# Half-height low products of the shared layer paired across two parts, and the refinement's second layer as products of rounded parts, in a kernel of attention, two feed-forward blocks and a routed iteration

## What is computed

```python
v, integrated = 0, x
for _ in range(2):                                   # NUM_ITER
    ctx = concat([integrated, v])
    shared_ctrl = gelu(ctx @ w_s1 + b_s1) @ w_s2 + b_s2          # shared layer, hidden 64
    x_shared, v_shared = inl(shared_ctrl, integrated, v, mu)
    hidden = gelu(ctx @ w1[expert] + b1[expert])                  # 2 of 8 experts, hidden 64
    ctrl = hidden @ w2[expert] + b2[expert]
    x_r, v_r = inl(ctrl, ...)                                     # weighted over the two
    x_next = sw * x_shared + (1 - sw) * x_r
    v_next = sw * v_shared + (1 - sw) * v_r
    halt = sigmoid(gelu(x_next @ w_h1 + b_h1) @ w_h2 + b_h2)
    refined = gelu(x_next @ w_f1 + b_f1) @ w_f2 + b_f2            # refinement, 128 -> 256 -> 128
    integrated = integrated + halt * refined * integration_weight
    v = v_next
```

## Time and profile before

| | us |
|---|---|
| median of 3 runs | 353.34 (353.13 to 353.79) |
| the profiled execution | 352.54 |
| its span in the profile | 350.8 |
| PE busy | 320.6 (91%), 1498 instructions |
| PEld busy | 225.9 (64%) |
| DVE busy | 276.4 (79%), 548 instructions |
| ACT busy | 194.8 (56%), 307 instructions |
| POOL busy | 35.4 (10%) |
| granted TensorE clock | 0.981 of full speed |
| chain that ended last, by engine | PE 68%, DVE 15%, ACT 7%, issue 5% |

### The profile page before, as it was taken

One profiled execution on the slowest core, in us unless ns is written; L12 is line 12 of the kernel. 1 busy time (PEld: TensorE's weight loads), 2 busy tenths in 40 slices (PEclk: granted clock), 3 DMA queues, 4 the chain that ended last, 5 costly groups with the idle time before them and its releaser, 6 DMA issues.

```text
span 350.8 us, 4318 instructions
## 1 busy us (share of the span) xinstructions
PE 320.6 (91%) x1498; PEld 225.9 (64%) x1498; DVE 276.4 (79%) x548; ACT 194.8 (56%) x307; POOL 35.4 (10%) x41
## 2 busy tenths in 40 slices
PE   4989999899898777896998999999999999999996
PEld 4654787445464454574675777777777777776763
DVE  0556767645757668969999999999997996999694
ACT  3500026285746274497778784866746846635743
POOL 0040020211111110709000100000000000000000
PEclk9989999999999679999999999999999999999999
DMA  7999930000000000000000100101000100000001
GB/s 266 421 429 298 325 153 0 0 2 2 0 2 0 0 1 2 0 0 2 1 0 0 33 0 2 30 0 30 2 1 0 32 1 0 32 0 0 32 0 60
DMA packets 11444, 18.91 MB, mean 54 GB/s; under 512 B 416, under 2 KB 8864, under 8 KB 10144
## 3 DMA queue, kind: packets, MB, share of 16 engines
q1 hardware_dynamic: 10848, 17.60, 14.5%
q0 software_dynamic: 576, 1.05, 1.8%
HBM read 16.55 MB, written 1.05 MB: 50 GB/s over the span
## 4 chain that ended last, share of the span: by engine, by line
PE 68%; DVE 15%; ACT 7%; issue 5%; POOL 2%; DMA 2%; SPq 0%; DVEq 0%; ACTq 0%; POOLq 0%
PE ps L1255 63%; DVE zz L860 3%; POOL lrs L381 2%; DVE lst L845 2%; PE ps L1352 2%; DMA ctxT<-in_ctxT 2%; PE ps L1331 1%; ACT hid L535 1%; DVE st L745 1%; ACT ring L483 1%; ACT L646 1%; DVE lmv L848 1%; DVE a L761 1%; PE ps L1437 1%; DVE kv L1144 1%
## 5 line engine op out<-in xcount | busy, mean ns | idle before, releaser
L1255 PE MATMUL ps<-hm_even,ew_hi 128*128 128x512 f32 (+1 forms) x160 | 51.0, 417 | 1.1 <-issue 1.1
L1255 PE MATMUL ps<-hm_odd,ew_hi 128*128 128x512 f32 (+1 forms) x164 | 51.6, 416 | 0.0
L1255 PEld LDWEIGHTS ps<-hm_odd,ew_hi 128*128 128x128 f32 (+1 forms) x164 | 28.7, 189 | 5.8 <-issue 0.5
L1255 PEld LDWEIGHTS ps<-hm_even,ew_hi 128*128 128x128 f32 (+1 forms) x160 | 27.9, 188 | 6.3 <-issue 1.2
L535 ACT ACTIVATE hid<-ps,pB 128x512 f32<-128x512 f32 x32 | 21.6, 687 | 13.4 <-PE ps L1255 12.8
L1255 PE MATMUL ps<-hm_odd,ew_lo 128*128 128x512 f32 (+1 forms) x80 | 28.3, 391 | 0.0
L1255 PE MATMUL ps<-hm_even,ew_lo 128*128 128x512 f32 (+1 forms) x80 | 28.3, 390 | 0.0
L860 DVE TENSOR_SCALAR zz<-ps,lmv,lrs 128x128 f32<-128x128 f32 x48 | 16.4, 404 | 9.4 <-POOL lrs L381 9.2
L381 POOL TENSOR_TENSOR lrs<-lve,mhalf 128x4 f32<-128x4 f32 x12 | 12.2, 1017 | 106.0 <-DVE lve L850 106.0
L1255 PE MATMUL ps<-x_hi,w1x_hi 128*128 128x512 f32 x40 | 18.9, 474 | 4.3 <-ACT ring L503 2.2
L945 DVE SCALAR_TENSOR_TENSOR ring<-ring,pB,hid 128x1024 f32<-128x1024 bf16 x16 | 20.5, 1282 | 2.0 <-ACT hid L535 1.3
(11 more groups left out here) (291 smaller groups left out, 739.4 us busy)
## 6 DMA issues: line engine op xcount, KB each, us to landing
ring<-in_fc1b SPq DMA_DIRECT2D x4, 1024.0 KB, 17.8
ring<-in_fc2a SPq DMA_DIRECT2D x4, 1024.0 KB, 8.9
packC<-in_packC SPq DMA_DIRECT2D x1, 1152.0 KB, 9.3
pB<-in_packB SPq DMA_DIRECT2D x1, 1141.5 KB, 10.1
ctxT<-in_ctxT SPq DMA_DIRECT2D x2, 512.0 KB, 6.7
xtok<-in_xtok SPq DMA_DIRECT2D x1, 1024.0 KB, 9.4
xT<-in_xT SPq DMA_DIRECT2D x1, 1024.0 KB, 11.4
a<-in_fc1a SPq DMA_DIRECT2D x1, 1024.0 KB, 13.4
```

What stands on the lines that cost most here:

```text
L1255: return pe.matmul(out, lhsT, rhs, start=start, stop=stop)
```

## The change

**Part one, from step 2 on (`PAIRED = 2`).** In the second part of a step (GATE in steps 2 and 3, ALPHA in steps 4 to 7) the ninth half-height product is left out. It is issued instead in BETA's `row_tiles`, right behind BETA's own, on the bottom half of the array and into the next group's shared bank. For that the bottom half needs the high part of the shared tile in rows 64 to 127, which before held only the low part. So ScalarE's two gelus of 128 rows become three of 64: `hsf` (full, rows 64 to 127, in the memory of `hsh`), `hs_hi` (rounded, rows 64 to 127, in a place of its own) and `hsh` (rounded, rows 0 to 63). VectorE's subtraction makes the low part in place from the first two. `hsu` rises twice a step, and `hsu_at(s)` gives its value after the last gelu of step s. BETA's `row_tiles` has two more waits: for the squashing of the group before, whose banks are written, and for `hsu`.

**Part two, refinements 4, 5 and 6 (`SPLIT`).** `refine1` writes each half of fh twice, rounded (`fh_hi`) and in full. VectorE subtracts (`refine_low`, behind `halt_low`, in steps 5, 6 and 7). `refine_b` makes six products of parts in place of two in full. The weights are split once, in step 4.

**Besides.** The full gelu of h1 covers its 32 rows alone; the four semaphores of GpSimd's accumulating transfers become one, and each transfer waits for the one before.

The diff, cut (allocations and the renaming of `xsum` left out):

```diff
+        SPLIT = range(NCH, STEPS - 1)
+        PAIRED = 2
+        def hsu_at(s):
+            return s + 1 + max(0, s + 1 - PAIRED)
...
                     if j == HT:
                         if s >= 1:
                             act.wait_ge(sem("hsl"), s)
-                        act.activation(hs, hid_bank(s, HT), ACT.Gelu, bias=W("bs1")).then_inc(sem("hs"), 1)
-                        if s >= 2:
+                        if s >= PAIRED:
 
                             act.wait_ge(sem("part_ps"), group(s - 1, 0))
-                        act.activation(hsh[:, s % 2, :], hid_bank(s, HT), ACT.Gelu, bias=W("bs1"))\
-                            .then_inc(sem("hsu"), 1)
+                            out, half = hid_bank(s, HT), slice(64, 128)
+                            act.activation(hsf[half, s % 2, :], out[half], ACT.Gelu, bias=W("bs1")[half])\
+                                .then_inc(sem("hs"), 1)
+                            act.activation(hs_hi[s % 2][half, :], out[half], ACT.Gelu, bias=W("bs1")[half])\
+                                .then_inc(sem("hsu"), 1)
+                            act.activation(hsh[0:64, s % 2, :], out[0:64], ACT.Gelu, bias=W("bs1")[0:64])\
+                                .then_inc(sem("hsu"), 1)
...
+                    if s in SPLIT:
+                        act.activation(fh_hi[:, j, :], bank[7 - j], ACT.Gelu, bias=W("bf1", j, j + 1))\
+                            .then_inc(sem("fhi"), 1)
                     act.activation(fh[:, j, :], bank[7 - j], ACT.Gelu, bias=W("bf1", j, j + 1))\
                         .then_inc(sem("fhg"), 1)
...
-                act.activation(h1, bank[7], ACT.Gelu, bias=W("bh1")).then_inc(sem("h1f"), 1)
+                act.activation(h1[32:64], bank[7][32:64], ACT.Gelu, bias=W("bh1")[32:64]).then_inc(sem("h1f"), 1)
...
+                if s == NCH:
+                    act.wait_ge(sem("hm"), (HT - 1) * (s + 1))
+                    act.activation(wf2_hi, W("wf2"), ACT.Copy).then_inc(sem("wf2"), 1)
...
+                if s >= PAIRED:
+                    dve.wait_ge(sem("hsu"), hsu_at(s) - 1)
+                    dve.tensor_tensor(hsh[half, s % 2, :], hsf[half, s % 2, :], hs_hi[s % 2][half, :].bitcast(F),
+                                      ALU.subtract).then_inc(sem("hsl"), 1)
...
+            def refine_low(s):
+
+                dve.wait_ge(sem("fhg"), 2 * s + 2)
+                dve.wait_ge(sem("fhi"), 2 * (s - SPLIT[0]) + 2)
+                dve.tensor_tensor(fh_lo[:, :, :], fh, fh_hi[:, :, :].bitcast(F), ALU.subtract).then_inc(sem("flo"), 1)
...
                 if s >= 1:
                     halt_low(s - 1)
+                if s - 1 in SPLIT:
+                    refine_low(s - 1)
...
                     mm(lo, w_hi[top, :], m[top, 1, 0, :], start=False, stop=not first)
-                    mm(hi, w_hi[bot, :], m[bot, 1, 0, :], start=False, stop=not first)
-                    return mm(sh, ws2_lo[top, o], h[top, :], start=first, stop=not first)
+                    last = mm(hi, w_hi[bot, :], m[bot, 1, 0, :], start=False, stop=not first)
+                    if paired and part == parts(s)[1]:
+                        return last
+                    if paired and rows_last:
+
+                        pe.wait_ge(sem("squash"), 2 * n)
+                        pe.wait_ge(sem("hsu"), hsu_at(s))
+                    last = mm(sh, ws2_lo[top, o], h[top, :], start=first, stop=not first)
+                    if paired and rows_last:
+                        p = parts(s)[1]
+                        mm(bank[3 * (n % 2)], ws2_lo[bot, p * D:(p + 1) * D], hs_hi[s % 2][bot, :], stop=False)
+                    return last
...
+                if s in SPLIT:
+                    pe.wait_ge(sem("wf2"), 2)
+                    pe.wait_ge(sem("flo"), s - SPLIT[0] + 1)
                 for j in range(2):
-                    last = mm(bank[7], W("wf2", j * 128, (j + 1) * 128), fh[:, j, :],
-                              start=j == 0, stop=j == 1)
+                    w = slice(j * 128, (j + 1) * 128)
+                    if s in SPLIT:
+                        mm(bank[7], wf2_hi[:, w], fh_hi[:, j, :], start=j == 0, stop=False)
+                        mm(bank[7], wf2_lo[:, w], fh_hi[:, j, :], start=False, stop=False)
+                        last = mm(bank[7], wf2_hi[:, w], fh_lo[:, j, :], start=False, stop=j == 1)
+                    else:
+                        last = mm(bank[7], W("wf2")[:, w], fh[:, j, :], start=j == 0, stop=j == 1)
                 last.then_inc(sem("f2_ps"), 1)
                 if s + 3 < STEPS:
-                    pe.wait_ge(sem("hsu"), s + 4)
+                    pe.wait_ge(sem("hsu"), hsu_at(s + 3))
```

More of the change, by code:

```diff
@@ L115, in build @@
         bank = [ps[:, i * CH:(i + 1) * CH] for i in range(8)]
+        hB_at = (nc.sbuf_base + 31) // 32 * 32
         hB_f = sb("hB", [128, 2 * FT * CH])
@@ L147, in build @@
         vtok = vtok_f.rearrange("p (b d) -> p b d", b=B)
+        wz_at = (nc.sbuf_base + 31) // 32 * 32
         wz = sb("wz", [128, 3 * CH])
@@ L206, in build @@
         hs = wz[:, 2 * CH:3 * CH]
+        hsh_at = (nc.sbuf_base + 31) // 32 * 32
         hsh = sb("hsh", [128, 2, CH], FR)
+        hsf = nc.alloc_sbuf_tensor_at("hsf", [128, 2, CH], F, offset=hsh_at)
+        hs_hi = tuple(nc.alloc_sbuf_tensor_at(n, [128, CH], FR, offset=at)
+                      for n, at in (("hs_hi_even", wz_at + 4 * 2 * CH), ("hs_hi_odd", zz_at + 4 * 3 * CH)))
         hm = (wz[:, 0:2 * CH].rearrange("p (k n) -> p k n", k=2),
@@ L238, in build @@
         wh2s = sb("wh2s", [128, 1], FR)
+        wf2_hi, wf2_lo = (placed(n, 2 * D, ring_at + 4 * (IDX0 + i * 2 * D)) for i, n in enumerate(("wf2_hi", "wf2_lo")))
+        fh_hi, fh_lo = (nc.alloc_sbuf_tensor_at(n, [128, 2, CH], FR, offset=at)
+                        for n, at in (("fh_hi", hB_at), ("fh_lo", zz_at)))
         xn_hi, xn_lo = placed("xn_hi", CH, ctxT_at + 4 * 3 * CH), placed("xn_lo", CH, zz_at + 4 * 2 * CH)
@@ L415, in _ @@
                 pool.wait_ge(sem("xi"), s + 1)
-                pool.dma_start(xT[:, ck(s)], xi[:, ck(s)], accum_op=ALU.add).then_inc(sem(f"xsum_{s}"), 16)
+                if s:
+                    pool.wait_ge(sem("xsum"), 16 * s)
+                pool.dma_start(xT[:, ck(s)], xi[:, ck(s)], accum_op=ALU.add).then_inc(sem("xsum"), 16)
         @block.scalar
@@ L516, in hidden_gelus @@
                             act.wait_ge(sem("hsl"), s)
-                        act.activation(hs, hid_bank(s, HT), ACT.Gelu, bias=W("bs1")).then_inc(sem("hs"), 1)
-                        if s >= 2:
+                        if s >= PAIRED:
                             act.wait_ge(sem("part_ps"), group(s - 1, 0))
-                        act.activation(hsh[:, s % 2, :], hid_bank(s, HT), ACT.Gelu, bias=W("bs1"))\
-                            .then_inc(sem("hsu"), 1)
+                            out, half = hid_bank(s, HT), slice(64, 128)
[6 more added lines that the diff above has]
+                        else:
+                            act.activation(hs, hid_bank(s, HT), ACT.Gelu, bias=W("bs1")).then_inc(sem("hs"), 1)
+                            act.activation(hsh[:, s % 2, :], hid_bank(s, HT), ACT.Gelu, bias=W("bs1"))\
+                                .then_inc(sem("hsu"), 1)
                     else:
@@ L998, in shared_halves @@
             def shared_halves(s):
+                half = slice(64, 128)
                 dve.wait_ge(sem("hs"), s + 1)
-                dve.wait_ge(sem("hsu"), s + 1)
-                dve.tensor_tensor(hsh[64:128, s % 2, :], hs[64:128, :], hsh[64:128, s % 2, :].bitcast(F),
-                                  ALU.subtract).then_inc(sem("hsl"), 1)
+                if s >= PAIRED:
+                    dve.wait_ge(sem("hsu"), hsu_at(s) - 1)
+                    dve.tensor_tensor(hsh[half, s % 2, :], hsf[half, s % 2, :], hs_hi[s % 2][half, :].bitcast(F),
+                                      ALU.subtract).then_inc(sem("hsl"), 1)
+                else:
+                    dve.wait_ge(sem("hsu"), s + 1)
+                    dve.tensor_tensor(hsh[half, s % 2, :], hs[half, :], hsh[half, s % 2, :].bitcast(F),
+                                      ALU.subtract).then_inc(sem("hsl"), 1)
             ln_stats("ffn", 0)
@@ L1198, in last_refine @@
                     link(dve.tensor_scalar(th[:, cut(i)], th[:, cut(i)], 1.0, iwh[:, 0:1], ALU.add, ALU.mult))
-                dve.wait_ge(sem(f"xsum_{NCH - 1}"), 16)
+                dve.wait_ge(sem("xsum"), 16 * NCH)
                 for i in range(2):
@@ L1214, in refine @@
                 else:
-                    dve.wait_ge(sem(f"xsum_{c}"), 16)
+                    dve.wait_ge(sem("xsum"), 16 * (c + 1))
                     dve.tensor_tensor(res[:, ck(c)], xT[:, ck(c)], rr, ALU.add).then_inc(sem("res"), 1)
@@ L1241, in _ @@
                     hidden_masked(s + 1, s + 2 < STEPS)
+                if s == NCH:
+                    dve.wait_ge(sem("wf2"), 1)
```

(4 more changed lines are left out.)

2 lines of the change are left out of this document (added).

## The result

The changed kernel takes 361.33 us (median of 6 executions, 358.96 to 362.19) beside 353.24 (352.53 to 356.08, also 6) for the one before: ratio 1.0186, interval 1.0140 to 1.0232. The forecast of 357.8 had the sign and missed the size; 361.33 lies above its range of 354.8 to 359.4. The profiled execution took 362.19, its span 360.0 against 350.8. In every ratio of this document the executions more than 1.5% above the fastest of their own kernel are left out (four of ten in delay_full, further down, at most two elsewhere).

What follows compares the result with a forecast made beforehand. TensorE was taken to bound up to step 6's tanh, VectorE from there to xn_lo and again at the end. Terms 1.90 + 1.26 + 1.26 = +4.42 us on the median 353.34 gave 357.8, range 354.8 to 359.4.

Steps and rivals of the forecast that it cites:

- Step 1's wait for the third gelu: Step 1: expand_3's weights load on TensorE waits for the last shared-tile gelu, a loss of 0.59 us.
- The h1s waits in steps 2 to 5: refine_b's halt product on TensorE waits for hsu, 0.50 us lost a step, +2.00 in all.
- I take 0.59 us more a step: ScalarE: three 64-row gelus for two full ones, each costing as much as a full one, 0.59 us more a step.
- Three slots in steps 3 to 5: TensorE: the second part's low product, paired with BETA's, saves a 0.23 us slot in each step, -0.69.
- Sum to the tanh: All terms from step 1 up to step 6's tanh, where TensorE sets the pace: +1.90 us.
- fh_lo in step 6: VectorE's added 128x1024 subtraction, in the stretch without a pause before xn_lo: +1.26 us.
- in step 7: The same VectorE subtraction, queued after h1s and ahead of all that the end needs: +1.26 us.
- The gelus of the first layer and the halting weights: Step 7: two added refine1 gelus on ScalarE, with halt_a beginning after two, just fit: nothing, 0.1 at the other end.
- The clock in the gap: Rival: TensorE's clock falls in step 7's 2.5 us gap ahead of refinement; products could double, +4.7, 362.5 us; chance 6%.

Runs made afterwards that it cites:

- delay_full: The kernel before, with the 32-row h1 gelu and one idle 128x1024 VectorE subtraction in step 7's turn, no pairing or split; ratio to before 1.0022.
- third_gelu: The changed kernel without the split and with the low products unpaired as before, its three 64-row gelus kept; ratio to the kernel before 1.0123.
- fill: The whole changed kernel plus eight idle TensorE products in step 7's gap ahead of refinement; ratio to the kernel before 1.0144.
- early_pair: The changed kernel without the split, its shared tile read by one full-height gelu and the rounded parts copied from that; 354.05 us, ratio to before 1.0009.
- split_only: The changed kernel without part one: two full gelus of the shared tile and the ninth half-height product as before; ratio to the kernel before 1.0131.

## Why the prediction was off

- **Step 1's wait for the third gelu**, forecast 0.59: right in place, 0.81 at step 2's tanh (third_gelu). The 0.70 between the halves accounts for half of the difference; the other half stays open.
- **The h1s waits in steps 2 to 5**, forecast 0.50 each: right in place, 0.47 to 0.65, together 2.36 for 2.00. "I take 0.59 us more a step" was the term mis-sized; it is 0.70, the distance seen where a gelu begins at other rows than the one before.
- **Three slots in steps 3 to 5**, -0.69: -0.70 and -0.71, measured from both sides. Sum to the tanh 2.46 to 2.54 for 1.90.
- **fh_lo in step 6**, +1.26, and **in step 7**, +1.26: both right in mechanism; 1.13 to 1.15 and 1.15.
- **The gelus of the first layer and the halting weights**, "it just fits": yes, fill shows 0.19 for all between xn_lo and h1s, and 0.10 to 0.13 of that is the 32-row gelu of h1, whose successor starts 0.70 behind it in the changed kernel; the variants without split and without a fall of the clock have it too.
- **The clock in the gap**, "the new gap of 2.5 us lies between solid stretches, like the second. If the clock fell ...: 6%". This step failed. The gap was forecast well (2.5, measured 2.44); the clock fell in both profiles of the change, +1.5 to +1.6 us. I had priced it at up to 4.7, with all 19 products at the lower level; it returns before they end. By the marks this term takes the result out of the range: on the median of 353.34, the 5.0 us of fill give 358.4 and the 6.5 of the change 359.9, above the range's 359.4. The error was in the evidence: one row of a 2.02 us gap at full clock, in step 1, was taken for a rule. The trace of before had a case that pointed the other way, a gap of 2.19 us that ends at 126.37, behind six us in which TensorE was busy 5.70, though mostly at the lower level (granted clock 0.52):

```profile
126.37 0.47 PE L1255 MATMUL ps<-x_hi,w1x_hi 128*128 128x512 f32 x1 [2.19 <-ACT ring L503]
```

```profile
126.37:130.37 4.00, 4.00 (x14) 3.13 (x15) 2.29 (x5) 3.48 (x5) 0.00 (x0) 0.63 0.00 0
```

  Fourteen profiles now stand side by side for step 7's gap ahead of refinement: in the eight with 0.35 to 1.60 us the clock stayed at 1.00, in the six with 1.87, 2.12, 2.21, 2.43, 2.44 and 2.45 it was 0.57 to 0.64 over the next four us. And step 1's 2.02 us gap, the one that I leant on, has the fall too in one of the profiles, early_pair's:

```profile
163.68:167.68 4.00, 3.92 (x9) 2.62 (x11) 3.90 (x5) 2.88 (x4) 3.46 (x4) 0.57 0.00 0
```

  The Trainium skill, TensorE: Matmul & The Clock Gate, HAM oscillation, says that waits between bursts can throttle TensorE again and again. The trace agrees in part: 0.57 after 2.44 us of idle time, but 1.00 after the 2.17 us that follow in the same step. By the rows above, the rival deserved more than 6%.
- **The rest**, 361.33 - 353.24 = 8.1 against 6.5: the work up to the first mark differs between executions by more than that, as its column shows, and the lowest executions of the two kernels are 6.4 apart. That the six executions of the change drew a worse set than the six of before is consistent with all runs; it is argued, not shown.

In sum: 4.42 forecast, 6.51 measured on the changed part. The 2.09 between them are 0.64 up to the tanh, nearly all of it the third gelu's size (3.17 - 2.59 = 0.58 in third_gelu), 1.49 from the clock, and 0.19 from the small things between xn_lo and h1s, less 0.23 on the two fh_lo.

## What to carry to other kernels

When a buffer has several readers, ask which of them releases it: the third reader of a PSUM tile cost 3.2 us over five steps here, while one reader and two copies from SBUF cost none. When a change lengthens the idle gap of TensorE ahead of a stretch that TensorE bounds, price the clock with it, also where the gap grows because TensorE got faster, and look through the whole trace for gaps of that length, not at one; eight idle products in the gap were enough to keep it. And a queue's order is a price of its own: the same subtraction cost 1.15 us behind h1s and nothing ahead of it.

## What was not expected of the hardware

- ScalarE: activations of 512 columns on the same rows start 0.59 apart, but 0.70 where the next begins at other rows (64 to 127, then 0 to 63: 218.97 to 219.67; 32 to 63, then all: 337.82 to 338.52).
- TensorE's clock: behind six us in which TensorE was busy throughout at 1.00, the gap ahead of refinement in step 7 kept it at up to 1.60 us (eight profiles) and lost it at 1.87 us or more (six), some 1.5 us of time each. That is no threshold: the last gap of the same step kept it at 2.17, 2.17 and 2.27 us and lost it at 2.18 (split_only). In step 1, where TensorE was busy 5.5 of the 6 us before, a gap of 2.0 us kept it in 13 of 14 profiles. Why equal gaps end differently no run here shows.
- The kernel before takes 352.11 to 357.67 us from execution to execution. The profiles differ in where the clock is low in the prologue, which no part of the steps causes. That the clock is the whole cause is not shown: of before's own executions one took 355.11 at a granted clock of 0.981, another 353.61 at 0.970.
